# Moving the w + 1 − 1 of a softplus from GpSimd to ScalarE, and a bias product with 64 rows instead of one

## The reference

```
xn = layernorm(x)
# Mamba, per sequence, 512 inner channels, 16 states per channel
x_s, z = split(rmsnorm(xn) @ in_proj_w.T)
u      = silu(conv4(x_s) + conv_b)
dt, B, C = split(u @ x_proj_w.T)
delta  = softplus(dt @ dt_proj_w.T + dt_proj_b)
h_t    = exp(delta_t * A) * h_{t-1} + delta_t * u_t * B_t
y_t    = sum over states of h_t * C_t
out    = x + xn + (y + u * D) * silu(z) @ out_proj_w.T + experts(xn)
```

## Time and profile before

| | |
|---|---|
| time, median of 3 runs | 2923.68 us (2920.98 to 2927.97) |
| time of the profiled execution | 2921.28 us |
| its span in the profile | 2919.5 us |
| mean granted clock of PE | 0.891 of full speed |
| busy: PE, DVE, POOL, ACT | 83%, 85%, 69%, 52% of the span |
| chain that ended last | PE 48%, POOL 16%, DVE 15%, issue 11%, ACT 4%, transfers 4% |

### The profile page before, as it was taken

One profiled execution on the slowest core, in us unless ns is written; L12 is line 12 of the kernel. 1 busy time (PEld: TensorE's weight loads), 2 busy tenths in 40 slices (PEclk: granted clock), 3 DMA queues, 4 the chain that ended last, 5 costly groups with the idle time before them and its releaser, 6 DMA issues.

```text
span 2919.5 us, 50661 instructions
## 1 busy us (share of the span) xinstructions
PE 2437.7 (83%) x14442; PEld 2049.5 (70%) x14442; DVE 2467.5 (85%) x3901; ACT 1504.8 (52%) x3675; POOL 2001.6 (69%) x1467
## 2 busy tenths in 40 slices
PE   2876655579999899999999989899898999997775
PEld 2864544458788778787778877788787777775554
DVE  6979777798899888898888898888898887998997
ACT  1444444455555555455555555555465554565553
POOL 3346999985777766677766777666676666777873
PEclk8757766779999999999999999999999999997776
DMA  7442432244565555464555565555564554542431
GB/s 219 120 106 80 155 104 75 75 143 129 161 180 148 158 168 156 143 189 142 163 162 148 160 174 158 155 167 147 159 174 137 168 163 147 175 119 53 78 75 36
DMA packets 316127, 406.46 MB, mean 139 GB/s; under 512 B 44296, under 2 KB 207496, under 8 KB 315800
## 3 DMA queue, kind: packets, MB, share of 16 engines
q1 hardware_dynamic: 284448, 359.49, 40.3%
q0 software_dynamic: 28144, 43.01, 8.1%
q10 hardware_dynamic: 3208, 0.19, 0.1%
HBM read 332.59 MB, written 78.39 MB: 141 GB/s over the span
## 4 chain that ended last, share of the span: by engine, by line
PE 48%; POOL 16%; DVE 15%; issue 11%; DMA 4%; ACT 4%; SPq 2%; ACTq 0%; DVEq 0%; POOLq 0%
PE HT L1246 9%; POOL h L468 7%; DVE h L1015 6%; PE G L1288 5%; PE G L1295 5%; PE FA L1205 4%; PE FB L1205 4%; PE G L1302 4%; DVE yT L1030 3%; DMA xraw<-in_x_dram 3%; PE FA L1172 3%; POOL xbuf L432 3%; PE FA L1311 2%; PE FB L1172 2%; POOL tmpA L476 2%
## 5 line engine op out<-in xcount | busy, mean ns | idle before, releaser
L468 POOL TENSOR_TENSOR h<-du,bbc 128x512 f32<-128x512 f32 x1024 | 1356.8, 1412 | 786.9 <-PE HT L1246 750.2
L1015 DVE TENSOR_TENSOR_SCAN h<-DA,carry,h 128x256 f32<-128x256 f32 x2048 | 1416.5, 733 | 196.1 <-ACT DA L716 83.5
L716 ACT ACTIVATE DA<-delta,alog 128x256 f32<-128x256 f32 x2048 | 891.4, 469 | 589.2 <-DVE h L1015 516.1
L1246 PE MATMUL HT<-ident,h 128*128 128x128 f32 x4096 | 687.8, 302 | 356.0 <-DVE yT L1030 329.1
L1246 PEld LDWEIGHTS HT<-ident,h 128*128 128x128 f32 x4096 | 514.9, 154 | 502.0 <-issue 359.1
L1030 DVE SCALAR_TENSOR_TENSOR yT<-HT,cT,yT 128x512 f32<-128x512 f32 x960 | 698.2, 727 | 187.8 <-PE HT L1246 187.3
L1288 PE MATMUL G<-xtT,W 128*128 128x128 f32 x2160 | 287.8, 290 | 0.0
L1288 PEld LDWEIGHTS G<-xtT,W 128*128 128x128 f32 x2160 | 274.5, 206 | 2.9
L1295 PE MATMUL G<-xtT,W 128*128 128x128 f32 x2160 | 263.8, 275 | 0.0
L1302 PE MATMUL G<-W,fill 128*128 128x256 f32 x1080 | 257.7, 381 | 3.3 <-DVE fill L991 3.3
L1295 PEld LDWEIGHTS G<-xtT,W 128*128 128x128 f32 x2160 | 252.8, 192 | 0.0
(11 more groups left out here) (169 smaller groups left out, 2694.7 us busy)
## 6 DMA issues: line engine op xcount, KB each, us to landing
W<-in_w_T_dram SPq DMA_DIRECT2D x405, 512.0 KB, 4.9
bbc<-b_dram SPq DMA_DIRECT2D x256, 256.0 KB, 5.2
xbuf<-fill SPq DMA_DIRECT2D x68, 258.0 KB, 8.5
W<-xbuf SPq DMA_DIRECT2D x135, 128.0 KB
xraw<-in_x_dram SPq DMA_DIRECT2D x64, 256.0 KB, 6.3
W<-in_x_dram SPq DMA_DIRECT2D x32, 256.0 KB, 7.1
out_dram<-tmpA SPq DMA_DIRECT2D x32, 256.0 KB
moe_dram<-fill SPq DMA_DIRECT2D x32, 256.0 KB
```

Of the source, the lines that this page charges most:

```text
L468: pool.tensor_tensor(h[:, v % RING], du[:, b, 2 * q:2 * q + 2, :], bbc[:, s // 2 % BRING, s % 2, :].unsqueeze(1).to_broadcast([P, 2, T]), ...
L716: i = act.activation(DA[:, v % 2, k, :], delta[:, b, c, :], ACT.Exp, scale=nega[:, c, s:s + 1])
L1015: i = dve.tensor_tensor_scan(h[:, v % RING, k, :], DA[:, v % 2, k, :], h[:, v % RING, k, :], carry[:, b, s, c:c + 1], ALU.mult, ALU.add)
L1246: i = pe.transpose(HT[:, k, c * P:(c + 1) * P], h[:, (2 * s + c // 2) % RING, c % 2, k * P:(k + 1) * P], ident[:, :])
```

## The change

ScalarE makes 1 + w and then subtracts 1, in two operations over all 1024 elements per partition, in slot 25 just ahead of the Ln; the second waits for the first through a new semaphore s_one, and it counts up s_wm, on which POOL's correction waits as before. POOL no longer has that operation, nor its wait for w. The subtraction takes its −1 from a one-column tile. The bias product reads rows 64 to 127 of dtT and xdbc: row 64 as before, and 63 rows of zeros against ones. Two more memsets at the start fill these (the counts that others wait for go from 10 to 12).

```diff
-        dtT = sb("dtT", [BIAS_ROW + 1, DI])
+        dtT = sb("dtT", [P, DI])
+        minus1 = sb("minus1", [P, 1])
-        xdbc = sb("xdbc", [BIAS_ROW + 1, T])
-        one_row = xdbc[BIAS_ROW:BIAS_ROW + 1, :]
+        xdbc = sb("xdbc", [P, T])
+        bias_rows = dtT[BIAS_ROW:P, :]
+        one_rows = xdbc[BIAS_ROW:P, :]
...
-            def exp_ready(j, b):
-                pool.wait_ge(s_et, number(j, b) + 1)
-
-            def w_minus_1(j, b):
-                pool.tensor_scalar(tmpA[:, :, :], tmpB[:, :, :], 1.0, -1.0, ALU.add, ALU.add).then_inc(s_wm, 1)
...
-            pool.memset(one_row, 1.0).then_inc(s_id, 1)
+            pool.memset(one_rows, 1.0).then_inc(s_id, 1)
...
+            pool.memset(bias_rows, 0.0).then_inc(s_id, 1)
...
+            pool.memset(minus1[:, :], -1.0).then_inc(s_id, 1)
...
-                    if nxt and due("wm", v):
-                        exp_ready(*nxt)
...
-                        if due("wm", v):
-                            w_minus_1(*nxt)
...
                 act.wait_ge(s_halo, 2 * n + 2)
+                act.activation(tmpA[:, :, :], tmpB[:, :, :], ACT.Identity, bias=1.0).then_inc(s_one, 1)
+                act.wait_ge(s_one, n + 1)
+                act.activation(tmpA[:, :, :], tmpA[:, :, :], ACT.Identity, bias=minus1[:, :]).then_inc(s_wm, 1)
                 act.activation(lnw, tmpB[:, :, :], ACT.Ln, bias=1.0).then_inc(s_ln, 1)
...
-                pe.matmul(dst, cb_row[:, c * P:(c + 1) * P], one_row, start=True, stop=False)
+                pe.matmul(dst, bias_rows[:, c * P:(c + 1) * P], one_rows, start=True, stop=False)
```

More of the change, by code:

```diff
@@ L166, in build @@
          s_route, s_tot, s_cnt, s_slot, s_disp, s_xt, s_xtr, s_xtT, s_h1, s_h3, s_th, s_a2, s_ha,
-         s_y2, s_yo, s_sc, s_mz, s_add, s_gate, s_iota, s_disp2) = [sem(n) for n in """
+         s_y2, s_yo, s_sc, s_mz, s_add, s_gate, s_iota, s_one, s_disp2) = [sem(n) for n in """
             s_par s_prep s_id s_x s_xres s_xn s_oacc s_tr s_xT s_xsmm s_zmm s_xs s_halo s_conv s_tu
@@ L172, in build @@
             s_route s_tot s_cnt s_slot s_disp s_xt s_xtr s_xtT s_h1 s_h3 s_th s_a2 s_ha
-            s_y2 s_yo s_sc s_mz s_add s_gate s_iota s_disp2""".split()]
+            s_y2 s_yo s_sc s_mz s_add s_gate s_iota s_one s_disp2""".split()]
         s_w = [sem(f"s_w{i}") for i in range(WSLOTS)]
@@ L508, in _ @@
             pool.wait_ge(s_id, 6)
-            pool.memset(one_row, 1.0).then_inc(s_id, 1)
+            pool.memset(one_rows, 1.0).then_inc(s_id, 1)
             pool.wait_ge(s_id, 7)
-            pool.memset(dtT[0:ROWS, :], 0.0).then_inc(s_id, 1)
+            pool.memset(dtT[0:BIAS_ROW, :], 0.0).then_inc(s_id, 1)
             pool.wait_ge(s_id, 8)
+            pool.memset(bias_rows, 0.0).then_inc(s_id, 1)
+            pool.wait_ge(s_id, 9)
             pool.memset(halo[:, :, :, :], 0.0).then_inc(s_id, 1)
+            pool.memset(minus1[:, :], -1.0).then_inc(s_id, 1)
             pool.memset(carry[:, :, :, :], 0.0).then_inc(s_id, 1)
@@ L520, in _ @@
             pool.tensor_tensor(yy[:, :, 0:EARLY * NT], vv[:, :, 0:EARLY * NT], mhalf, ALU.pow).then_inc(s_rstd, 1)
-            exp_ready(0, 0)
-            w_minus_1(0, 0)
             correction(0, 0)
@@ L745, in _ @@
             act.dma_start(gwT[:, :, :], gwT_d.rearrange("(k p) e -> p k e", p=P)).then_inc(s_par, 16)
-            act.wait_ge(s_id, 10)
+            act.wait_ge(s_id, 12)
             act.dma_start(dtT[0:R, :], dtT_d).then_inc(s_par, 16)
@@ L1064, in _ @@
                 dve.tensor_scalar(inT[:, k, :], inT[:, k, :], nw[:, k:k + 1], None, ALU.mult).then_inc(s_prep, 1)
-            dve.wait_ge(s_id, 10)
+            dve.wait_ge(s_id, 12)
             dve.tensor_tensor(cwd[:, :, :, :].rearrange("p c k i -> p (c k) i"),
@@ L1218, in transpose_c @@
                 n = number(j, b)
-                pe.wait_ge(s_id, 10)
+                pe.wait_ge(s_id, 12)
                 pe.wait_ge(s_xdbc, n + 1)
```

## The result

| | before | after |
|---|---|---|
| time, median of 5 runs | 2923.68 us (2920.35 to 2927.97) | 2945.54 us (2936.33 to 2948.96) |
| profiled execution, and its span | 2921.28 us, 2919.5 | 2948.96 us, 2947.2 |
| busy: PE, DVE, POOL, ACT | 83%, 85%, 69%, 52% | 83%, 84%, 64%, 53% |
| mean granted clock of PE | 0.891 | 0.885 |

The ratio of the times is 1.0071, with a 95% interval of 1.0051 to 1.0092: the changed kernel is slower by 0.7%, 22 us. Its profiled execution is the slowest of its five; it is 27.7 us above the profiled execution of before.

What follows compares the result with a forecast made beforehand. No engine is full; DVE's scans wait for POOL in the dispatch and for ACT in the expert steps. −14.8 + 19.5 + 19.8 + 1.3 + 0.5 + 2.2 + 4.8 = +33.3 us gave 2955 us, range 2920 to 2976.

Steps and rivals of the forecast that it cites:

- ACT's two operations: Slot 25 ahead of the Ln: 2.2 us more per block, none hidden where DVE's scan already waits for ACT.
- The second rival: ACT's work is hidden, as ACT is idle for 48% of the span; only POOL's gain stands, 2891 us; chance 0.04.
- POOL in the dispatch: Steps 1 to 4, where POOL's queue is the path: gain 3.64 + 0.05 us each, −14.8 us.
- The thirteen steps without a branch: Within steps 6 to 27: DVE 2.2 us later, less 0.36 + 0.35 of POOL waits; +1.5 each, +19.5 us, clock apart.
- The nine with a branch: Steps of 6 to 27 with a loop branch behind: ACT's delay stays, +2.2 each, +19.8 us, clock apart.
- The case in which the branch absorbs ACT's delay too: The nine branch steps: the branch wait's end moves only partly with DVE's arrival, leaving +0.9 us each; not taken.
- PE's clock: Idler PE at half clock in steps 6 to 27: 0.3 us for thirteen, 0.1 for nine; +4.8, bounds 0 and 19.
- Rival 4: A colder PE: each event pays 0.86 us extra, and the nine a second late wait: 2969 to 2977 us; chance 0.08.
- The bias product: On PE at the convolution: 64 rows pay the same surcharge as one row, 0 us; bounds 0 and 50 us gain.
- the first rival: The 64 rows shed the bias product's surcharge of 0.39 us per channel group: 2905 us, faster; chance 0.10.
- The small terms: Step 5 ahead of the expert tiles +1.3 us, last three steps +0.5, step 0 +2.2.
- the likeliest case: Case 5, the forecast itself: 2955 us, with a range of its own of 2938 to 2970; chance 0.70.

Runs made afterwards that it cites:

- e8: Changed kernel with one row in the bias product, ACT's two operations one slot later behind the next decays, POOL's correction in slot 28: 2899.34 us, ratio 0.9926.
- e7: Kernel before, with ACT's two operations for blocks 2 to 5 only (made in steps 1 to 4) and POOL's for all others: 2905.14 us, ratio 0.9938.
- e3: Changed kernel with w + 1 − 1 left out on every engine; POOL's correction subtracts w from itself: 2891.20 us, ratio 0.9889.
- e1: Changed kernel with the one-row bias product of before, so ACT's two operations alone: 2945.99 us, ratio 1.0084.
- e5: Changed kernel with the +1 operation made twice on ACT, each with its own wait: 2965.82 us, ratio 1.0150.
- e2: Kernel before with the 64-row bias product alone, POOL keeping its operation: 2925.72 us, ratio 1.0009.
- e6: Kernel before with the bias product over all 128 rows, identity as weights and the bias column as data: 2871.30 us, ratio 0.9820.

## Why the prediction was right, step by step

**ACT's two operations: right.** The forecast had 1.06 and 1.18 us and 2.2 in all; the rows have 1.05, 1.15 and a shift of 2.13 of the table load and of the scan behind the decays. The reading of the earlier trace rows, that ACT is the last to arrive exactly there though half idle, is what e8 shows: with the same operations on the same engine behind the decays the loss of 40 us is gone. The second rival, that ACT's idle half hides them, fell for this place.

**POOL in the dispatch: right, a little small.** −16.3 us in steps 1 to 4 against −14.8, −16.6 in e7. The block shown gained 3.79 us, where the term had 3.69; ACT's delay of 1.1 us lay inside the wait for h, as the step had it.

**The thirteen steps without a branch: right in the sum.** Forecast 1.5 + 0.3 = 1.8 us each; measured 22.6 / 13 = 1.74, and the block shown has 1.8. Its terms are 2.03 for ACT, −0.71 for POOL and 0.47 for PE; in the mean of the thirteen the last two are −0.60 and 0.39. The prediction read −0.71 in one step and took it for all: four of the thirteen show only one of the two waits for POOL, or none. e3 warns of this term in another way too: taken away alone, the waits gave 4.5 us in the thirteen steps instead of 9, and DVE's waits for PE grew by 0.30 us. So POOL's gain and PE's loss are not independent, and that the two terms were each right in size is in part luck.

**The nine with a branch: right in kind.** The loss that arises 16 us ahead of the branch stays whole, and only the one just ahead of it, PE's 0.95, is absorbed (3.82 to 2.88; in the mean of the nine, 0.39 more of waiting for PE and 0.52 less at the branch). Forecast 2.3 each, measured 17.5 / 9 = 1.94 (both sums from the starts of w), and 17.4 in e1. The case in which the branch absorbs ACT's delay too, 0.9 each, didn't come. In e5, though, the third added operation left nothing in these nine steps, so the rule that ACT's delay passes a branch whole is shown for the change and not for every delay.

**PE's clock: there, and smaller than its bound.** The sixteen matmuls of L1288 take 3.62 instead of 3.21 us in the block of the earlier trace rows. Over the 22 steps they take 1.95 to 3.62 us before, 2.96 in the mean, and 3.06 to 3.62, 3.52 in the mean, after. So the prediction's "this happens at each event now" was wrong: in five of the 22 steps before they took 1.95 us (in one of them, read from 2499.9 to 2501.8 us, the granted clock is 1.00), behind the same 1.31 and 1.82 us of idling as where they took 3.62. Behind 3.44 us of idling instead of 1.32, in the changed kernel, none of them is under 3.06 us. There the windows show the clock. Its columns are the window and its length, the busy time of PE, PEld, DVE, ACT and POOL, the granted clock (0.57 and 0.50), the DMA share and GB/s:

```profile
1440.00:1448.00 8.00, 6.07 (x30) 5.42 (x31) 8.00 (x13) 3.74 (x13) 6.63 (x4) 0.57 0.59 207
1532.00:1535.50 3.50, 3.50 (x18) 3.18 (x18) 3.50 (x6) 1.21 (x5) 3.17 (x3) 0.50 0.20 67
```

In the thirteen it costs 0.47 us in the block shown and 0.39 in the mean, against 0.3; in the nine 0.95 in the block shown and 0.39 in the mean, and the branch wait takes it. Rival 4 would have needed 0.86 in all of them and nothing absorbed.

**The bias product: right, 0.** 0.63 and 1.93, as with one row, and e2 has a ratio of 1.0009 with an interval of 0.9999 to 1.0020. The argument from 49 rows held for 64. e6 shows that the first rival named a real gain, of 42 us in 31 blocks, at the wrong row count.

**The small terms.** Step 5: +0.7 against +1.3. Last blocks: 0.0 against +0.5. Start: +3.2 against +2.2, and −0.6 in e1, so nothing more than its spread can be said of it.

**Where the number was off.** 2955 was forecast and 2945.54 measured, inside the range of 2938 to 2970 that went with the likeliest case. The terms add up to +33.3, the profiled execution has +27.7, of which the 22 steps are 4 too few and the dispatch 1.5 too much of a gain; the median has +21.9, since the profiled execution was the slowest of its five. Before the result nothing could tell this last part, but it means that the sum was half as large again as the change of the medians, and that the forecast is right in path and sign more than in size.

## What to carry to other kernels

What an added operation costs is decided by what is queued behind it: 2.2 us on an engine that is half idle cost 1.8 us each time ahead of a table load and a decay that DVE waits for, and 0.4 us of waiting one slot later, behind that decay, which POOL's relief paid for. Before work is moved, look up for each stage which engine arrives last at the consumer; here POOL's relief was worth 16 us in four steps, and in the other twenty-two a few us that one execution can't tell from none. A product with few rows in a stream of full ones was made cheaper by using all 128 rows, and not by going from 1 to 64.

## What the runs showed of the hardware

- Products of 32-bit data with 1, 49 or 64 of the array's rows pay about 0.2 us, and so do the full ones behind a bias product: 0.62 and 1.93 us with 1 and with 64 rows, 0.43 and 1.73 with 128; 1.06 with 49 rows for four passes, 0.86 with 128. The Trainium skill, "TensorE: Matmul & The Clock Gate", section on why this matters for your kernels, says that a single product with 32 rows takes the time of one with 128. In this stream of mixed products the rows disagree: the ones with part of the rows took longer.
- The length of PE's idling does not by itself say when the full clock is back. Behind the same idle times of 1.31 and 1.82 us the same sixteen matmuls took 1.95 to 3.62 us in the kernel before; behind 4.53 us of idling they took 2.84 to 3.62 in e5 (mean 3.32), behind 3.44 us 3.06 to 3.62 in the changed kernel (mean 3.52). In e5's block the granted clock is 0.50 up to 1455 us and 1.00 from 1456 us on, inside the group; what sets the moment was not tried.
- POOL's w + 1 − 1 with its two steps of arithmetic took 3.64 to 4.25 us, where its subtraction of two tiles of the same size takes 2.36.
- The wait at a loop's branch on DVE, 3.82 us, took up a delay of 0.95 us that arose 3 us ahead of it (at 1536.36, where DVE came to the branch at 1538.8) and not the 2.0 us that arose 16 us ahead of its end. Over the nine branches it averages 3.56 us before and 3.04 in the changed kernel.
